# A recommender tower: the Gram of each pass moves to the head of PE's next run, weights are loaded late, and one gather gate is changed

## The reference

```python
e = stack([tbl_f[ids[:, f]] for f in range(26)], axis=1)      # 2048 x 26 x 128
combined = concatenate([dense[:, None, :], e], axis=1)         # 2048 x 27 x 128
interactions = einsum('bfd,bgd->bfg', combined, combined)      # a Gram matrix per sample
z = concatenate([dense, interactions[:, iu, ju]], axis=1)      # upper triangle, 351 pairs
h = concatenate([z, dense], axis=1)
h = maximum(h @ W_top1 + b_top1, 0)                            # 607 -> 512
h = maximum(h @ W_top2 + b_top2, 0)                            # 512 -> 256
y = h @ W_top3                                                 # 256 -> 1
```

## Time and profile before

| | us |
|---|---|
| median of 3 runs | 380.98 |
| lowest and highest | 379.82, 381.19 |
| profiled execution | 382.01 |
| its span, first to last instruction | 380.2 |
| PE busy in it | 341.6 |
| DVE, POOL, ACT busy | 243.5, 250.9, 147.8 |

### The profile page before, as it was taken

How to read it: one execution, slowest core, us unless ns; L and a number is a source line. 1 busy time by engine, 2 the same in 40 slices (tenths; PEclk the granted TensorE clock), 3 DMA queues, 4 the chain that set the end, 5 groups by cost and what they waited for, 6 DMA issues and landing times.

```text
span 380.2 us, 15163 instructions
## 1 busy us (share of the span) xinstructions
PE 341.6 (90%) x6472; PEld 327.4 (86%) x6472; DVE 243.5 (64%) x308; ACT 147.8 (39%) x305; POOL 250.9 (66%) x265
## 2 busy tenths in 40 slices
PE   0478754999989999999999999999999999999996
PEld 0468644899979998999989998999989997999996
DVE  3779817499257946589267936598367926697133
ACT  2356422444325224434335224434334224523431
POOL 6788778767777777677766776767766776661000
PEclk9989888799999999999999999999999999999999
DMA  7978972333233332243232332333333422110000
GB/s 180 248 182 215 278 233 56 82 79 107 79 97 77 84 104 69 70 103 83 83 91 71 94 93 71 74 97 77 83 92 75 105 84 62 49 47 14 0 2 1
DMA packets 20607, 36.05 MB, mean 95 GB/s; under 512 B 7698, under 2 KB 9490, under 8 KB 20596
## 3 DMA queue, kind: packets, MB, share of 16 engines
q0 software_dynamic: 8192, 16.79, 18.1%
q1 hardware_dynamic: 12260, 18.84, 17.8%
q10 hardware_dynamic: 144, 0.26, 0.3%
HBM read 35.87 MB, written 0.01 MB: 94 GB/s over the span
## 4 chain that ended last, share of the span: by engine, by line
PE 83%; DMA 6%; issue 5%; DVE 2%; POOL 2%; ACT 1%; SPq 0%; DVEq 0%; POOLq 0%
PE oh_ps L671 39%; PE work_ps L697 14%; PE work_ps L744 11%; PE tr_ps L682 7%; PE work_ps L786 5%; DMA emb<-table,ids_sb 4%; PE work_ps L709 3%; POOL emb L313 2%; DVE onehot L523 1%; DMA gram<-table 1%; PE work_ps L726 1%; PE work_ps L718 1%; PE oh_ps L786 1%; PE work_ps L722 1%; PE work_ps L775 1%
## 5 line engine op out<-in xcount | busy, mean ns | idle before, releaser
L313 POOL DMA_INDIRECT emb<-table,ids_sb x256 | 250.0, 977 | 92.2 <-issue 70.5
L523 DVE TENSOR_TENSOR onehot<-ids_b,rows_ps 125x1024 fp32r<-125x1024 int32 (+1 forms) x160 | 189.7, 1239 | 28.5 <-PE oh_ps L671 23.4
L671 PE MATMUL oh_ps<-onehot,hi 125*128 125x256 f32 x656 | 167.8, 294 | 17.8 <-DVE lo L536 13.2
L671 PE MATMUL oh_ps<-onehot,lo 125*128 125x256 f32 x656 | 163.2, 287 | 0.0
L671 PEld LDWEIGHTS oh_ps<-onehot,hi 125*128 125x128 f32 x656 | 128.0, 195 | 20.8 <-issue 15.1
L671 PEld LDWEIGHTS oh_ps<-onehot,lo 125*128 125x128 f32 x656 | 128.4, 196 | 0.0
L374 ACT ACTIVATE emb_t<-oh_ps 128x256 f32<-128x256 f32 x80 | 51.2, 642 | 105.8 <-PE oh_ps L671 104.2
L697 PE MATMUL work_ps<-emb_t 128*32 128x26 f32 x4096 | 53.1, 197 | 9.5 <-issue 5.6
L697 PEld LDWEIGHTS work_ps<-emb_t 128*32 128x32 f32 x4096 | 45.8, 111 | 17.3 <-issue 14.3
L563 DVE SCALAR_TENSOR_TENSOR top_in<-work_ps,top_in 128x512 fp32r<-128x512 f32 x14 | 9.6, 687 | 56.3 <-ACT top_in L417 56.3
L390 ACT ACTIVATE emb_t<-tr_ps 128x512 f32<-128x512 f32 x64 | 43.4, 746 | 4.7 <-PE tr_ps L682 4.7
(11 more groups left out here) (108 smaller groups left out, 238.1 us busy)
## 6 DMA issues: line engine op xcount, KB each, us to landing
ids_b<-ids_t SPq DMA_DIRECT2D x39, 256.0 KB, 3.5
emb<-table,ids_sb POOLq DMA_INDIRECT x256, 2.6
emb_t<-table SPq DMA_DIRECT2D x3, 448.0 KB
dense_sb<-dense_t SPq DMA_DIRECT2D x8, 128.0 KB
emb<-table SPq DMA_DIRECT2D x2, 448.0 KB
gram<-table SPq DMA_DIRECT2D x2, 448.0 KB
pairs<-table SPq DMA_DIRECT2D x2, 448.0 KB
gram<-w SPq DMA_DIRECT2D x1, 768.0 KB, 4.6
```

Of the source, the lines that this page charges most:

```text
L313: pool.indirect_dma_start(emb[:, i, s, :], None, tables[t], bass.IndirectOffsetOnAxis(ap=ids_sb[:, i, t:t + 1], axis=0),).then_inc(gathere ...
L523: dve.tensor_tensor(onehot[:, n % ONEHOT_BUFFERS, 0:h, :], ids_b[0:CHUNK_ROWS, u, :].unsqueeze(1).to_broadcast([CHUNK_ROWS, h, PAIR]), row ...
L671: mm = pe.matmul(oh_ps[u % 2][:, 0, :], part[:, CHUNK_BASE[u] + chunk, :], onehot[:, (HALVES * u + s) % ONEHOT_BUFFERS, c, :], start=chunk ...
```

## The change

Four edits, on three engines.

PE's loop runs nine times. A run begins with the four Gram calls of the pass before, each under its own test `b > 0`, so that the first run steps over them one by one. All the rest of the body stands under a test `b < STEPS`, so that the ninth run does only the Gram calls. The two waits that stood ahead of the loop (constants made, two tables ready) are now at the head of that body and are met in every run. The order of PE's work is the same.

Because `gram_products` now stands in a run where all engines' counts are one pass on, ACT raises `gram_moved` by 4 at its start and the two waits on it add 4. The first run would not need it; the waited values are otherwise the same.

SP issues the weights later: ids of pass 1 first, then it waits for all of tile 1's gathers of the first pass and for `lo_made` 10, then w1's main part, its dense part twice, w2, and the two vectors.

POOL's gate of group (1, 2) is the fourth group of transposes of tile 0 in place of the first half of unit 3.

```diff
@@ sync
             load_dense(0)
+            sp.wait_ge(onehot_ready, 2 * HALVES)
+            spread_ids(1, 0)
+
+            for g in range(NG):
+                sp.wait_ge(gathered[1][g], 16 * GROUP)
+            sp.wait_ge(lo_made, ONE)
+            sp.dma_start(w1_raw, w1[D:D + 3 * P, :].rearrange("(k p) n -> p k n", p=P)).then_inc(w1_ready, 16)
             sp.dma_start(w1_dense, w1[0:D, :]).then_inc(w1_dense_ready, 16)
             sp.dma_start(w1_twice[:, :], w1[D + 3 * P:D + 3 * P + D, :]).then_inc(w1_dense_ready, 16)
+            sp.dma_start(w2_raw, w2.rearrange("(k p) n -> p k n", p=P)).then_inc(w2_ready, 16)
             sp.dma_start(b2_sb[:, :], b2.rearrange("(a n) -> a n", a=1).to_broadcast([P, H2])).then_inc(vectors_ready, 16)
             sp.dma_start(w3_sb[:, :], w3.rearrange("(a n) o -> a (n o)", a=1).to_broadcast([P, H2]))\
               .then_inc(vectors_ready, 16)
-
-            sp.wait_ge(onehot_ready, 2 * HALVES)
-            spread_ids(1, 0)
-            sp.wait_ge(lo_made, ONE)
-            sp.dma_start(w1_raw, w1[D:D + 3 * P, :].rearrange("(k p) n -> p k n", p=P)).then_inc(w1_ready, 16)
-            sp.dma_start(w2_raw, w2.rearrange("(k p) n -> p k n", p=P)).then_inc(w2_ready, 16)
@@ gpsimd
                 elif (i, g) == (1, 2):
-                    pool.wait_ge(onehot_used, b * UNIT_HALVES + (HALVES * 3 + 1))
+                    pool.wait_ge(transposed, b * (2 * NG) + NG)
@@ scalar
             act.sem_inc(slots_moved, AHEAD)
+            act.sem_inc(gram_moved, 2 * AHEAD)
@@ tensor
-            pe.wait_ge(consts_made, len(row_i) + 2)
-
...
                 if (i, u) == (1, 0):
-                    pe.wait_ge(gram_moved, b * 4 + 1)
+                    pe.wait_ge(gram_moved, b * 4 + (2 * AHEAD + 1))
...
                 if n == 0:
-                    pe.wait_ge(gram_moved, b * 4 + 4)
+                    pe.wait_ge(gram_moved, b * 4 + (2 * AHEAD + 4))
...
-            pe.wait_ge(lo_made, 2)
-            with pe.Fori(0, STEPS) as b:
-                unit(b, 0)
-                transposes(b, 0, 0)
...
-                with pe.If(b > 0):
-                    first(b - 1, 1)
+            with pe.Fori(0, STEPS + 1) as b:
                 for i in range(2):
                     for u in range(2):
-                        gram_products(b, i, u)
+                        with pe.If(b > 0):
+                            gram_products(b - 1, i, u)
+                with pe.If(b < STEPS):
+                    pe.wait_ge(consts_made, len(row_i) + 2)
+                    pe.wait_ge(lo_made, 2)
+                    unit(b, 0)
+                    transposes(b, 0, 0)
...
+                    with pe.If(b > 0):
+                        first(b - 1, 1)
```

More of the change, by code:

```diff
@@ L791, in second @@
                         mm.then_inc(h2_ready, 1)
-            pe.wait_ge(lo_made, 2)
-            with pe.Fori(0, STEPS) as b:
-                unit(b, 0)
-                transposes(b, 0, 0)
-                transposes(b, 0, 1)
-                with pe.If(b > 0):
[L800 to L827, removed]
-                    first(b - 1, 1)
@@ L829, in _ @@
+            with pe.Fori(0, STEPS + 1) as b:
                 for i in range(2):
                     for u in range(2):
-                        gram_products(b, i, u)
+                        with pe.If(b > 0):
[5 more added lines that the diff above has]
+                    transposes(b, 0, 0)
+                    transposes(b, 0, 1)
+                    with pe.If(b > 0):
+                        turn(b - 1, 0)
+                        turn(b - 1, 1)
+                    unit(b, 1)
+                    unit(b, 2)
+                    transposes(b, 0, 2)
+                    transposes(b, 0, 3)
+                    with pe.If(b > 0):
+                        turn(b - 1, 2)
+                        turn(b - 1, 3)
+                    unit(b, 3)
+                    unit(b, 4)
+                    with pe.If(b > 1):
+                        pe.wait_ge(pairs_act, b * len(TURNS_ACT) + AHEAD)
+                        second(b - 2)
+                    unit(b, 5)
+                    with pe.If(b > 0):
+                        turn_pairs(b - 1)
+                    unit(b, 6)
+                    unit(b, 7)
+                    transposes(b, 1, 0)
+                    transposes(b, 1, 1)
+                    unit(b, 8)
+                    with pe.If(b > 0):
+                        first(b - 1, 0)
+                    unit(b, 9)
+                    transposes(b, 1, 2)
+                    transposes(b, 1, 3)
+                    with pe.If(b > 0):
+                        first(b - 1, 1)
```

## The result

The changed kernel took 379.65 us in the median (378.07 to 381.76), the kernel before, on the same chips, 381.18 (379.82 to 383.27), 20 executions each. The ratio is 0.9964, 95% interval 0.995 to 0.9979: about 1.4 us faster by the ratio (1.5 between the medians). Forecast were 4.2 us. The sign and the range held; the size was a third of what was forecast. Some executions take a few per cent longer whatever the kernel; all ratios here compare executions without that, so that a ratio can differ from the quotient of two medians. The profiled execution after took 381.57 us (span 379.7), at the high end of its twenty; so the two traces, 382.01 and 381.57, account for 0.4 us and the rest lies within the scatter between executions.

The account below looks back on a forecast made before the run. PE was taken to bound the kernel, with page fetches and a late gather holding its first pass. Terms -6.6 + 1.6 + 0.3 + 0.5 = -4.2 us gave 376.8 us against a median of 380.98, range 372.8 to 382.4.

Parts of the forecast that it names:

- What bounds the kernel, and the pages: PE bounds; holes in its first Gram are instruction page fetches, about 3.9 us each; the loop then stays loaded.
- (b): Skips do not load Gram pages, first Gram stalls: 379.1, chance 0.12; worse form, loop not staying whole: 412, chance 0.03.
- Part 1, the start: The first run's four skips fetch the Gram's pages while PE waits for tables; gathers shift by about 0.
- S: Start of PE's first unit after the skips, expected 12.7 to 25.3 us, taken as 18.5.
- D: Shift of the start chain, S - 16, forecast 2.5 us; S up to 16 costs nothing.
- Rival (a): Slow fetch at the start: both fetches under load take 6.3 us extra or more, S = 26; 382.4, chance 0.14.
- Part 2, the late weights: First pass: weights moved behind the gathers free the last gather; next unit starts at 62.5 instead of 69.1, -6.6 us.
- next: Start of PE's first product after the first Gram: 69.14 us before, forecast about 62.5.
- Rival (c): First pass: w1 lands in 7.6 us, not 4.6, behind its followers and the gathers: +3, 379.8, chance 0.09.
- Part 3, the tests: Tests in PE's Gram cost 0.2 us a pass, +1.6 over eight passes, and +0.3 for the ninth run's jump.
- Rival (d): Tests cost 0.3 us each inside a Gram already starved: +4.8, 381.6, chance 0.05.
- Part 4, POOL: The gate saves 0.4 a pass in Grams 4 to 6, 0.7 once; late POOL costs Grams 2 and 3 1.2 each: +0.5.

Follow-up runs that it names:

- one_test_2: The changed kernel with one test around all four Gram calls in place of four: 381.64 us, ratio 1.0008 to the kernel before.
- loop_only: The kernel before with only PE's loop of nine runs and its tests (tensor and scalar parts): 381.24 us, ratio 1.0017.
- weights_only: The kernel before with only SP's late weights: 384.14 us, ratio 1.0100.
- quiet_start: The changed kernel with the loads of tables 2 to 9 held back until PE has passed the skips: 380.98 us in one execution.
- gate_only: The kernel before with only POOL's third gate earlier: 378.60 us, ratio 0.9954.
- after_again_2: The changed kernel unchanged, measured again on a chip where the kernel before takes over 500 us: 516.6 us, ratio 1.0245 to the kernel before there.

## Why the prediction was right or wrong, step by step

- **What bounds the kernel, and the pages.** Right. The blocks of the first Gram were page fetches; the four skips moved them to the start (q8 at 2.5, 9.3, 18.0), the loop of nine still stays loaded (seven packets in all), and the rule of the Trainium skill (page "Runtime: NRT & Kernel Launch", section "Instruction fetch mechanics") that a taken branch out of the window forces a fetch did not hold for this loop. The worse form of (b) fell. Its mild form, that skips don't load the pages, is false for four skips of a page and true for one jump over all (one_test_2).
- **Part 1, the start.** The step that failed first is the choice "I take S = 18.5, a little under the middle". It puts the two fetches under load at 6.8 us each; the tests' rows have 7.15 and 8.56, about twice the 3.9 read from the kernel before, and S was 21.22. The first fetch, which falls where the load begins, took 3.49. The slack worked out behind it was nearly right: with this S, D = S - 16 is 5.2, and the table half that ended at 23.14 ended at 28.39, +5.25. By D - 2.4 the gathers shift by 2.8; the seventeenth went from 25.51 to 29.18, +3.7, since POOL began it 0.8 us after the table half, which the working left out. The last of tile 1 went from 47.08 to 50.60, +3.5 where 0 was forecast: 2.8 of it from the fetches' size, 0.7 from the slack. Rival (a) had this mechanism and half came true.
- **Part 2, the late weights.** Forecast: the gather begun at 47.08 lands at 49.7, the first copy is done at 58.2, next at 62.5. Measured: begun 50.60, landed 3.62 later at 54.22, w1 issued 54.35, landed 58.97, copy from 62.30, next at 67.13. Of the missing 4.6 us, 3.5 are the later gather, 1.0 its landing (3.62, not the median 2.6, though nothing of the weights moved beside it). The durations of the w1 chain behind it were right: 4.6, and 3.3 from the rounding's start to the copy's. So -6.6 became -2.0. The step also credited the edit wrongly: "does not wait" was true of the gather and worth nothing, since w1 then came as late as ACT had been without the edit (loop_only 58.97, changed kernel 58.99; next 67.10 and 67.13), and alone the edit costs 3.8 us, which no rival had: with the Gram's fetches unmoved, the weights beside them lengthen each (weights_only). Rival (c), w1 landing in 7.6, didn't come: 4.62.
- **Part 3, the tests.** Undersized. Forecast 0.2 a pass from 0.1 a test; measured 0.4 a pass, twice (7.32 to 7.76; 6.81 to 7.24), and 0.4 in the last Gram with 0.24 "issue" behind it, so 0.64 for the ninth run where 0.5 was summed. At 0.13 a test it lies in the low half of the bounds 0 to 0.3. The saving of 0.1 at the jump back wasn't seen. Rival (d) at 0.3 was too high, its sense right. The 0.4 was measured in passes in which POOL has idle time; if it held in all, this would be some 1.5 us more than forecast (0.2 in each of seven passes, 0.14 in the last).
- **Part 4, POOL.** Right in both directions. The gate is worth 0.5 us in each of the passes 4 to 6 (forecast 0.4), 1.8 to 2.4 us alone. POOL late: Grams 2 and 3 are 8.29 and 8.29 where before had 7.04 and 7.33, +1.25 and +0.96 (forecast +1.2 each); POOL's idle time at the gate inside them is gone, as forecast. But these differences hold part 3's tests too, so that the lateness alone is less, 0.85 and 0.56 if the tests take their 0.4 there. Whether the single gain of 0.7 "as POOL catches up" came can't be told apart.
- **The sum.** Forecast -6.6 + 1.6 + 0.3 + 0.5. By the traces: start -2.0; pass 1 another -0.8, with its Gram 8.47 against 8.48 and its first unit 1.1 shorter by the granted clock, a term that the forecast put at nothing; passes 2 and 3 +2.0, POOL's lateness and the tests; 4 to 6 -0.3, gate against tests; the last +0.7. Together -0.5 in this pair, -1.5 between the medians, so that terms under 1 us are known only for this pair of executions. The 3.7 us between -4.2 and -0.5 are the start's 4.6, with 0.9 gained back on all that follows. So what failed is the size of the start's gain, 2.0 for 6.6: the page fetches under load took too long and the late weights brought nothing beside the loop.

## What to carry to other kernels

Where a loop is long in instructions, read the instruction queue's packets: here the first run pays 3 to 4 us for each page of 256 instructions, 7 to 9 beside loads that fill the DMA engines (share 1.05); so fetches belong where both the engine and the queues are idle, and as few as will do (half of the stage skipped beat all of it, 377.56 against 379.65 us). To see what a late start waits for, look at the engine's own tests and waits too: the chain named a table that PE didn't need. A transfer that is put off to relieve another must be followed to its own consumer; here it put one delay in place of another. An edit that moves an engine's instructions is priced with its tests in the densest stretch, here 0.13 us each and every pass, against a gain that comes once.

## What the runs showed of the hardware

- A jump of PE over a page that isn't loaded takes 3.04 us at a DMA share of 0.15, 5.89 at 0.81 (quiet_start), 7.15 and 8.56 at 1.05 and 1.04 (changed kernel); I had expected load to matter less for a single packet than for a gather's 128.
- Jumps of one page each load the pages jumped over; a single jump over four pages doesn't (one_test_2).
- The start of a gather by POOL breaks PE's dense issue for about 0.5 us: the Gram of b = 5 takes 7.32 us with six gathers beginning in it, that of the last pass 4.66 with none. Which gathers fall in the Gram is worth 1.8 to 2.4 us of 380 by one gate (gate_only).
- On some chips the same program has breaks of 0.5 us after every one to four matmuls in places, and takes over 500 us (after_again_2); that gathers cause these isn't shown.
- The same unit of PE takes 3.12 us at a granted clock of 0.56 and 2.01 at 1.00 (kernel before and changed kernel, behind the first Gram).
